# Two output halves, or two projection tiles, in one interleaved group of matmuls (attention and mixture-of-experts layer, 8 cores)

## What is computed

```python
xn = layernorm(x)                                  # x: 4 x 4096 x 1024
q, k, v = xn @ Wq.T + bq, xn @ Wk.T + bk, xn @ Wv.T + bv      # 16 heads of 64
q, k = rope(rmsnorm(q)), rope(rmsnorm(k))
pattern = square(q @ k.T / 64) * causal            # no softmax
s = xn + (pattern @ v) @ Wo.T
logits = xn @ gate_w.T + gate_b                    # 8 experts, the best 2 kept
gate = softmax(top2(logits))
g = silu(sum_e gate[e] * (xn @ expert_w[e] + expert_b[e]))
out = x + s * g
```

## Time and profile before

| | |
|---|---|
| median of 2 runs | 2439.51 us (2433.81 to 2445.22) |
| the profiled execution | 2433.23 us |
| its span on the slowest core | 2431.7 us (all cores 2419.8 to 2431.7) |
| granted TensorE clock, mean of the span | 0.712 to 0.739 by core |
| busy shares: TensorE, VectorE, ScalarE, GpSimd | 71%, 44%, 32%, 19% |
| matmuls, weight loads | 6768, 6768 |

### The profile page before, as it was taken

The page is one execution under the profiler, slowest core; times in us unless marked ns, Lnnn a source line. Parts: engine busy times, 40 slices in busy tenths (PEclk is TensorE's granted clock), DMA queues, the critical chain, the costliest instruction groups (busy, mean ns, idle before and its releaser), DMA issues.

```text
span 2431.7 us, 24581 instructions; the slowest of 8 cores (2419.8 to 2431.7 us)
## 1 busy us (share of the span) xinstructions
PE 1714.5 (71%) x6768; PEld 572.9 (24%) x6768; DVE 1074.4 (44%) x1636; ACT 767.6 (32%) x914; POOL 470.9 (19%) x322
## 2 busy tenths in 40 slices
PE   0003777787756878888888888787368778687785
PEld 0001333332321111111111111123123233233232
DVE  1013665566535455454545454542363343333333
ACT  0002444554434555555555555551000000000000
POOL 0000444553451111111111111110000200300203
PEclk9856798898885555555555555559679889899897
DMA  9996223123351011010101010017213443534443
GB/s 186 115 118 111 87 96 113 56 97 100 117 114 69 25 29 45 10 46 9 44 9 46 7 48 5 22 42 218 100 57 117 160 137 119 173 128 141 150 136 104
DMA packets 145103, 213.02 MB, mean 88 GB/s; under 512 B 57288, under 2 KB 86984, under 8 KB 143440
## 3 DMA queue, kind: packets, MB, share of 16 engines
q1 hardware_dynamic: 139104, 186.26, 24.5%
q0 software_dynamic: 5872, 25.20, 8.4%
HBM read 186.30 MB, written 67.11 MB: 104 GB/s over the span
## 4 chain that ended last, share of the span: by engine, by line
PE 36%; DMA 23%; DVE 15%; issue 9%; ACT 7%; POOL 3%; another core or an unknown queue 3%; SPq 3%; DVEq 0%; ACTq 0%; POOLq 0%
PE p L947 9%; PE p L705 9%; DMA s_abf<-webf 9%; PE p L759 9%; DMA s_af<-x 8%; ACT s_abf L719 5%; PE p L423 4%; DVE s_abf L734 4%; DVE s_abf L724 4%; PE p L611 2%; PE p L808 2%; POOL s_af L993 1%; POOL s_af L996 1%; DMA s_af<-sinw 1%
## 5 line engine op out<-in xcount | busy, mean ns | idle before, releaser
L719 ACT ACTIVATE s_abf<-p 128x1024 bf16<-128x1024 f32 x480 | 491.3, 1024 | 437.3 <-PE p L759 394.6
L947 PE MATMUL p<-s_abf 128*128 128x512 bf16 x2048 | 498.6, 405 | 130.3 <-DMA s_abf<-webf 79.4
L705 PE MATMUL p<-s_abf 64*128 64x512 bf16 x1280 | 389.2, 596 | 151.3 <-DVE s_abf L724 39.5
L759 PE MATMUL p<-s_abf 128*64 128x512 bf16 x1280 | 408.0, 632 | 33.2 <-DVE s_abf L780 33.0
L958 DVE SCALAR_TENSOR_TENSOR s_af<-p,s_g_all,s_af 128x512 f32<-128x512 f32 x256 | 190.0, 749 | 276.2 <-PE p L947 275.8
L947 PEld LDWEIGHTS p<-s_abf 128*128 128x128 bf16 x2048 | 205.1, 103 | 414.5 <-issue 213.9
L728 POOL TENSOR_TENSOR s_abf<-s_abf 128x1024 bf16<-128x1024 bf16 x80 | 151.4, 1892 | 773.0 <-DVE s_abf L724 773.0
L744 DVE TENSOR_TENSOR s_abf<-s_abf,s_masks 128x1024 bf16<-128x1024 bf16 x256 | 170.8, 690 | 193.3 <-POOL s_abf L728 103.0
L423 PE MATMUL p<-s_abf 128*128 128x512 bf16 x768 | 195.7, 409 | 19.3 <-DVE s_af L460 16.7
L611 PE MATMUL p<-s_abf 128*128 128x512 bf16 x512 | 141.3, 426 | 68.2 <-DVE s_tiny L532 34.7
L705 PEld LDWEIGHTS p<-s_abf 64*128 64x128 bf16 x1280 | 79.8, 100 | 449.4 <-issue 449.3
(11 more groups left out here) (73 smaller groups left out, 1086.0 us busy)
## 6 DMA issues: line engine op xcount, KB each, us to landing
s_abf<-webf SPq DMA_DIRECT2D x32, 2048.0 KB, 9.4
s_af<-x SPq DMA_DIRECT2D x48, 512.0 KB, 4.5
webf<-we POOLq DMA_DIRECT2D x8, 2048.0 KB, 75.9
vsp<-s_abf SPq DMA_DIRECT2D x32, 256.0 KB, 2.1
xnsp<-s_abf SPq DMA_DIRECT2D x64, 128.0 KB, 1.8
ksp<-s_abf SPq DMA_DIRECT2D x8, 1024.0 KB, 4.6
s_abf<-vsp SPq DMA_DIRECT2D x8, 1024.0 KB, 6.7
s_abf<-ksp SPq DMA_DIRECT2D x8, 1024.0 KB, 5.3
```

Source lines behind the costliest of these rows:

```text
L705: _sp=sp, _ws=wsl: E.matmul(_sp[:, _u * QG:(_u + 1) * QG], kT_w[_ws].ap(_kb * 128, (_kb + 1) * 128, 64 * _u, 64 * _u + 64), qT_sl[_sl].ap( ...
L719: E.activation(_pat.ap(0, 2 * QG), _sp[:, 0:2 * QG], AF.Square),
L759: (lambda E, _u=u: E.matmul(p01[64 * _u:64 * _u + 64, _u * QG:(_u + 1) * QG], v_w[_ws].ap(_kb * 128 + _u * 64, _kb * 128 + _u * 64 + 64), ...
L947: _pp=pp, _s=esl: E.matmul(_pp[:, 0:HW], xnT_dh.ap(_ki * SO + _rc * 128, _ki * SO + (_rc + 1) * 128), we_r[_s].ap(_ki * D + _h * HW, _ki * ...
```

## The change

Three places get groups of 16 matmuls, interleaved one by one between two banks, in place of two groups of 8.

- `fuse_proj`: the first stages of two neighbouring projection tiles become one node. Its matmuls alternate between the two tiles, it waits for all that either of them waited for (both banks too), and its one semaphore increment comes after the sixteenth matmul. It is called for the k tiles and for the q tiles.
- Wo: both halves of a chunk are one node that writes pf2 and pf3; the two halves' matmuls alternate, so that neighbours have the same stationary block.
- Experts: the same, with pf2 and pf3 for even chunks, pf4 and pf5 for odd ones.

The number of matmuls, and all other operations, stay. The code still asks for every matmul in full, with its stationary operand. By the made-up costs a fused node counts 16 x 400 ns.

```diff
+        def fuse_proj(tiles):
+            for i in range(0, len(tiles) - 1, 2):
+                ea, fa, ra, wa = tiles[i][0]
+                eb, fb, rbb, wb = tiles[i + 1][0]
+                fz = [f for pair in zip(fa, fb) for f in pair]
+                tiles[i][0] = (ea, fz, list(dict.fromkeys(ra + rbb)),
+                               wa + wb)
+                tiles[i + 1][0] = []
...
+                fuse_proj(tiles)
                 emit_interleaved(tiles)
...
-            for half in range(NHO):
-                pp, kk = pf[2 + half % 2], f"pf{2 + half % 2}"
-                fns = []
-                for hp in range(C2):
-                    fns.append(lambda E, _hp=hp, _rc=rc, _h=half, _pp=pp,
-                               _zr=zr: E.matmul(
+            fns = []
+            for hp in range(C2):
+                for half in range(NHO):
+                    fns.append(lambda E, _hp=hp, _rc=rc, _h=half,
+                               _pp=pf[2 + half % 2], _zr=zr: E.matmul(
                         _pp[:, 0:HW],
                         _zr.ap(_hp * 128, (_hp + 1) * 128),
                         woT.ap(_hp * D + _h * HW, _hp * D + (_h + 1) * HW),
                         start=(_hp == 0), stop=(_hp == C2 - 1)))
-                b.group("tensor", fns, reads=[zr.k(), woT.k()], writes=[kk])
+            b.group("tensor", fns, reads=[zr.k(), woT.k()],
+                    writes=["pf2", "pf3"])
+            for half in range(NHO):
+                pp, kk = pf[2 + half % 2], f"pf{2 + half % 2}"
...
-                    for half in range(NHO):
-                        pi = 2 + 2 * (rc % 2) + half % 2
-                        pp, kk = pf[pi], f"pf{pi}"
-                        fns = []
-                        for ki in range(KI):
+                    pi0 = 2 + 2 * (rc % 2)
+                    fns = []
+                    for ki in range(KI):
+                        for half in range(NHO):
                             fns.append(lambda E, _ki=ki, _rc=rc, _h=half,
-                                       _pp=pp, _s=esl: E.matmul(
+                                       _pp=pf[pi0 + half], _s=esl: E.matmul(
...
-                        b.group("tensor", fns,
-                                reads=xnd_keys + [we_r[esl].k()],
-                                writes=[kk])
+                    b.group("tensor", fns,
+                            reads=xnd_keys + [we_r[esl].k()],
+                            writes=[f"pf{pi0}", f"pf{pi0 + 1}"])
+                    for half in range(NHO):
+                        kk = f"pf{pi0 + half}"
```

More of the change, by code:

```diff
@@ L953, in build_program @@
                                 start=(_ki == 0), stop=(_ki == KI - 1)))
-                        b.group("tensor", fns,
-                                reads=xnd_keys + [we_r[esl].k()],
-                                writes=[kk])
+                    b.group("tensor", fns,
[3 more added lines that the diff above has]
+                        kk = f"pf{pi0 + half}"
                         b.op("vector", lambda E, _a=ar, _h=half, _rc=rc, _e=e,
-                             _pp=pp, _ac=accr: E.scalar_tensor_tensor(
+                             _pp=pf[pi0 + half], _ac=accr:
+                             E.scalar_tensor_tensor(
                                  _ac.ap(_a * D + _h * HW,
```

## The result

The changed kernel takes 2499.2 us in the median (before in the same comparison: 2437.5). The ratio is 1.0232, 95% interval 1.0192 to 1.0271: slower by 2.3%, some 57 us. The medians, 62 us apart, are of all runs, while the ratio leaves out those in which a die was granted a lower clock than the other and took longer. I had said 2480, within 2400 to 2530, slower.

A forecast was written before the change was run, and what follows sets the result against it. It took expert runs to be bound by columns streamed, plus waits; 0 + 12 + 1 + 11 + 22 = +46 us on 2433.2 gave 2479, stated as 2480 with the median's offset; 8-in-10 range 2400 to 2530.

The forecast's parts named there:

- Weight loads and banks: 0: All fused matmuls: load count stays 6768, loads lie beside matmuls, alternating banks costs nothing; 0 us.
- The clock rival: Experts: alternating two banks leaves TensorE at 1.2 GHz, losing 410 us there, 2850 us or more in all; chance 3%.
- My bound from above for alternation: Fused matmuls: at most 0.01 us for each of 3584, 36 us; the prediction took 0.
- The skew stays: 0: Experts: the even chunks stay one chunk ahead, so 32 matmuls (6.9 us) still cover a weight load; 0 us.
- the sign: Whole kernel: whether the change makes it slower or faster than before; slower was forecast, +46 us.
- The rival's price of 79 us: Experts: fused chains fall into program order and the 79.4 us of weight waits go, giving 2400 us; chance 12%.
- a margin of 0.4 us of made-up cost: Experts' start, planner's costs: 1.8 us against 1.4 us decides that the even chunks again run one chunk ahead.
- Wo: +11: Wo stage: both copies wait for the sixteenth matmul, 1.15 us per chunk, about half hidden in waits; +11 us.
- Experts: +12 and +1: Experts: 12 waits for VectorE at changes of group grow 1.0 us each, +12; one more L958 at the end, +1.
- Projections: +22: Projections: later hand-off between pairs of tiles, 17 us, plus 5 us behind x loads; +22 us, bounds 0 and 60.
- the step that I priced at 17: Projections: some 20 of 48 pairs, paced by their own chain, start 0.85 us later each; 17 us.
- +5 for the x loads alone: Projections: at stalls behind x loads, bones or rotT matmuls queue behind 3.45 us of matmuls, not 1.73; +5 us.

The follow-up runs named there:

- e4: The changed kernel with the same 16-matmul nodes, but the first bank's 8 matmuls before the second bank's 8; ratio 1.0195 (+48 us) against the kernel before.
- e7: The kernel before, with only the planner edited so that the experts' matmul groups are planned in program order, no wait added; ratio 0.9633, 89 us faster.

## Why the prediction was right

- *Weight loads and banks: 0.* Held: 6768 loads, 0.216 us per matmul, and e4 without sharing or alternation has the same trace. The clock rival is out: 0.89 against 0.90 in the experts. The Trainium skill, page "TensorE: Matmul & The Clock Gate", section "A second HAM failure mode: psum-queue depth-cycling", tells of a bf16 kernel whose cycling through banks in each iteration brought short idle times and a clock that went back and forth, at a cost in throughput. No such cost shows here: the trace has the banks alternate at every matmul with the dense run unchanged. My bound from above for alternation counted 3584 fused matmuls; there are 768 + 256 + 2048 = 3072, so it should have been 31 us, and the 0 that I took is untouched.
- *The skew stays: 0.* Held, and it is the step on which the sign hung. The waits of 2.2 to 3.0 us are there, 26 of them, and e7 shows that the mechanism is the one named: without the skew they vanish. The rival's price of 79 us was too low for that case: program order took 97.5 us off the experts of the kernel before and 107.5 off those of the changed one (651.6 to 544.1), less 7 and 8 us of longer tail. It left out what the clock gives back with the waits. That the skew stayed hung on a margin of 0.4 us of made-up cost, as I had said, so the sign was not sure beforehand.
- *Wo: +11.* The mechanism held, the size was off: 18.7 measured. The gap is 1.36 us and not 1.15, because the hand-offs took 0.51 us, not 0.3. And nearly nothing of it went into the waits for z and the stores: the last nine chunks had no such wait to fill, and the waits for z, 7.0 us before, are still 6.4.
- *Experts: +12 and +1.* Measured 20.6, and the tail -1.3. What is left for the pair of banks is about 10, close to the 12. The other 10 came from a step I didn't take: I played the planner for TensorE's queue and not for SyncE's, where a 2 MB load moved in front of a 512 KB one. The restart that I read as 0.14 us after an L958 is 0.18 by the numbers that stand beside it; this changes nothing in the term.
- *Projections: +22.* Measured +14 against the same chip. The pairs without v groups stand 0.58 us further apart, under my 0.7 to 1.25, and only 7 or 8 steps are of that kind, so the step that I priced at 17 gives some 4 us. I had said that the delay fits in where v groups stand between; most of the measured loss lies there and at the transposes, in waits for VectorE that I had put at +5 for the x loads alone. That 22 and 14 are near each other is in part luck.

Two terms too small and one too large made 46 where 57 was measured (52, when the stages of this list are added): Wo and the experts with the tail were 14 us under, the projections 8 us over, and the errors partly cancel. The interval for the time was met with room, the single terms less well.

## What to carry to other kernels

Sharing a stationary block was worth nothing here, where the load lies under the matmul before it; look at the start-to-start time of a dense run (here 0.216 us against a load of 0.098) before grouping for it. What a bigger group does cost can be read beforehand: count the banks, and add copy and hand-offs wherever the next group needs the bank that was just filled. And where a planner orders the queues, look at every queue it orders, and at how many matmuls lie between the release of a buffer and the wait for its refill. That count was 32 of a possible 64 in both kernels, and was worth more than the whole change. A bigger node also changes the orders that such a planner makes: one swap in SyncE's queue was half of the experts' loss.

## What was not expected of the hardware

- A 512 KB load issued 2.2 us after a 2 MB load took 9.6 us where such loads took 4.1 in the median, and so at each change of group. With the 2 MB load 10.4 us ahead, in the kernel before, it was there in under 4.2 us.
- From TensorE's last matmul to the start of a copy on VectorE it was 0.25 us, on ScalarE 0.15 us, and from VectorE's end to TensorE's start 0.26 us in the Wo stage; the restart at the earlier trace rows was 0.14 to 0.18 us.
